# Gated cross-attention and expert mixture in one kernel: weight splits ahead of the context, late GpSimd splits, new work orders

## What is computed

```
q = LN(x) @ Wq;  k = ctx @ Wk;  v = ctx @ Wv          (ctx: 8 x 750 x 512; 8 heads of 64)
a = softmax(q k^T / 8) v, per head                     (scores of 224 x 750 per head)
x = x + tanh(g0) * (a @ Wo + bo)
y = LN(x);  l = y @ gate_w^T + gate_b;  l = l * rsqrt(mean(l^2) + eps) * rms_w
g = top softmax(l / 0.5) entry;  n = g / (g + 1e-6)
x = x + tanh(g1) * n * sum over 8 experts of (gelu(y @ w1[e] + b1[e]) @ w2[e] + b2[e])   (hidden 1024)
```

## Time and profile before

| | |
|---|---|
| runs | 1887.07, 1889.46, 1889.43 us; median 1889.43 |
| profiled execution | 1885.9 us, of which 1884.1 us are the span of the trace |
| DVE, ACT, POOL busy | 71%, 43%, 63% |
| PE, weight loads busy | 97%, 87% |
| mean granted PE clock | 0.99 |

### The profile page before, as it was taken

One profiled execution on the slowest core, in us unless ns is written; L12 is line 12 of the kernel. 1 busy time (PEld: TensorE's weight loads), 2 busy tenths in 40 slices (PEclk: granted clock), 3 DMA queues, 4 the chain that ended last, 5 costly groups with the idle time before them and its releaser, 6 DMA issues.

```text
span 1884.1 us, 32919 instructions
## 1 busy us (share of the span) xinstructions
PE 1821.5 (97%) x10360; PEld 1647.3 (87%) x10360; DVE 1328.9 (71%) x2247; ACT 812.7 (43%) x1570; POOL 1184.9 (63%) x901
## 2 busy tenths in 40 slices
PE   6999999999999869999999999999999999999998
PEld 6999999999999758888888888887888888888887
DVE  6777777777776776766766667579766676676667
ACT  4767666766766543332323323233223233232322
POOL 5525354352544468877777777867777777777742
PEclk9999999999999979999999999999999999999999
DMA  5011111021110213121121211213311112112111
GB/s 174 17 32 59 34 37 55 21 67 29 42 43 13 81 33 122 62 67 56 56 67 45 67 56 56 68 53 116 106 50 62 59 53 67 55 56 66 46 46 51
DMA packets 51804, 110.38 MB, mean 59 GB/s; under 512 B 12953, under 2 KB 25241, under 8 KB 51745
## 3 DMA queue, kind: packets, MB, share of 16 engines
q1 hardware_dynamic: 51744, 109.63, 18.2%
HBM read 98.61 MB, written 11.01 MB: 58 GB/s over the span
## 4 chain that ended last, share of the span: by engine, by line
PE 85%; DVE 9%; issue 3%; ACT 3%; DMA 0%; DVEq 0%; ACTq 0%; SPq 0%
PE bank L683 30%; PE scores L658 28%; PE bank L537 15%; PE scores L601 4%; PE bank L611 4%; PE bank L624 4%; DVE xs L777 1%; DVE neg_max L860 1%; DVE queries L841 1%; ACT queries L1057 1%; DVE acc L944 1%; PE bank L544 1%; DVE probsT L777 0%; PE scores L719 0%; DVE values L777 0%
## 5 line engine op out<-in xcount | busy, mean ns | idle before, releaser
L683 PE MATMUL bank<-w2s,hs 128*128 128x512 f32 x2688 | 621.8, 390 | 5.0 <-DVE acc L944 5.0
L683 PEld LDWEIGHTS bank<-w2s,hs 128*128 128x128 f32 x2688 | 504.3, 188 | 109.5 <-DVE acc L944 7.0
L658 PE MATMUL scores<-xs,w1s 128*128 128x448 f32 x2688 | 562.1, 368 | 4.2 <-DVE h_sum L923 4.2
L658 PEld LDWEIGHTS scores<-xs,w1s 128*128 128x128 f32 x2688 | 507.5, 189 | 49.0 <-issue 2.8
L923 DVE TENSOR_TENSOR h_sum<-scores,h_sum 128x448 f32<-128x448 f32 x448 | 267.2, 620 | 192.2 <-PE scores L658 191.8
L944 DVE TENSOR_TENSOR acc<-bank,acc 128x512 f32<-128x512 f32 x434 | 295.8, 687 | 123.8 <-PE bank L683 114.6
L1183 ACT ACTIVATE h_full<-h_sum,b1T 128x448 f32<-128x448 f32 x256 | 170.9, 668 | 316.9 <-DVE h_sum L923 306.6
L777 DVE TENSOR_TENSOR hs<-h_full,hs 128x448 fp32r<-128x448 f32 x256 | 237.0, 926 | 50.6 <-ACT hs L1184 50.6
L1057 ACT ACTIVATE h_sum<-scores 128x448 f32<-128x448 f32 x64 | 34.9, 545 | 489.9 <-PE scores L658 489.8
L1244 POOL TENSOR_SCALAR probs<-probs,row_inv 112x750 f32<-112x750 f32 x64 | 140.5, 2195 | 164.4 <-DVE row_inv L866 164.4
L1339 POOL CAST w1s<-w_stage 128x768 fp32r<-128x768 f32 x64 | 68.6, 1072 | 182.9 <-PE scores L658 182.9
(11 more groups left out here) (112 smaller groups left out, 2123.8 us busy)
## 6 DMA issues: line engine op xcount, KB each, us to landing
w_stage<-in_L_ffn_w SPq DMA_DIRECT2D x128, 512.0 KB, 3.5
ctx_raw<-in_ctx SPq DMA_DIRECT2D x8, 752.0 KB, 4.6
ctx_raw<-in_ctx SPq DMA_DIRECT2D x7, 748.0 KB, 4.6
xa<-in_x SPq DMA_DIRECT2D x16, 224.0 KB, 2.7
xres<-in_x SPq DMA_DIRECT2D x16, 224.0 KB, 2.7
x_scratch<-xres SPq DMA_DIRECT2D x16, 224.0 KB, 2.3
xt_scratch<-yT SPq DMA_DIRECT2D x16, 224.0 KB, 2.9
x_raw<-xt_scratch SPq DMA_DIRECT2D x4, 896.0 KB, 6.1
```

The source lines that it names most:

```text
L658: mm = pe.matmul(mb[BANK_OF[name]][:, 0:TH], w1s[j % 2][:, s, W_OF[name], kc, :], xs[:, i, m, kc, :], start=n == 0, stop=n == 5)
L683: mm = pe.matmul(bank[:, :], hs[j % 2][:, s, ht, t * P:(t + 1) * P], w2s[j % 2][:, m, ht, :], start=n == 0, stop=n == 5)
```

## The change

1. `N0` stands ahead of `C0.0` and `C0.1` in `HEAD_PLAN`; the rest of the head is reordered.
2. Each context half is loaded as two pairs of column blocks with a semaphore each; a pair is waited for alone.
3. `POOL_PIECES` is (3, 4, 5, 6, 7): ACT and DVE split the first value weights (piece 2), POOL the second key weights (piece 3). POOL begins only when all four context splits of batch 0 and all three splits of the other engines are done. PE waits for each piece at its first use.
4. `BODY_PLAN` and `END_PLAN` are reordered.
5. Between the passes: `POOL_LOWS` = 4, so DVE makes four of the seven lo parts, POOL the last three in step (1, 0, 0), between `w1_part` and `split_w2`. The seven results are spread over steps (1, 0, 0) to (1, 0, 3) by `RESULTS`, and each step's `w2` load follows the first result in it.
6. The gate's third part moves from step j = 2 to j = 3, after sum 1; its Exp moves to product 6 of step 2.

```diff
+RESULTS = {(1, 0, 0): {4: 0, 6: 1}, (1, 0, 1): {3: 2}, (1, 0, 2): {3: 3, 6: 4}, (1, 0, 3): {3: 5, 6: 6}}
+POOL_LOWS = 4
...
-    C0.0 N0 C0.1 L0.0 L0.1 A0.0 N1 K0.0.0 A0.1 K0.1.0 X0 X1 C1.0 N2 C1.1 Q0.0 K0.0.1 N3 N4 V0.0 S0.0 N5 S0.1 R0.0
-    Q0.1 N6 V0.1 V0.2 N7 R0.1 S1.0 M0.0 V0.3 V0.4 K0.1.1 V0.5 S1.1 M0.1
+    N0 C0.0 C0.1 L0.0 L0.1 A0.0 A0.1 K0.0.0 C1.0 N1 X0 C1.1 X1 N2 K0.1.0 K0.0.1 Q0.0 K0.1.1 S0.0 N3 N4 V0.0 Q0.1
+    S0.1 S1.0 R0.0 N5 V0.1 N6 V0.2 M0.0 M0.1 V0.3 V0.4 R0.1 V0.5 N7 S1.1
...
-    D<7 K1.0.0 T0.0 R1.0 Q1.0 R1.1 K1.1.0 T0.1 T0.2 M1.0 S2.0 S2.1 O<0 D0 M1.1 P0 R2.0 T1.0 L<1.0 K1.0.1 O<1 A<1.0
...
-    M7.0 T6.2 S>0.0 R7.1 S>0.1 K>0.1.1 Q>0.1 M7.1 P6 D6 R>0.0 V>0.4 T7.0 T7.1 M>0.0 T7.2 V>0.5 R>0.1 S>1.0 P7
+    D<7 R1.0 K1.0.0 T0.0 R1.1 Q1.0 K1.1.0 T0.1 T0.2 M1.0 S2.0 S2.1 O<0 D0 P0 M1.1 R2.0 L<1.0 A<1.0 T1.0 K1.0.1
...
+    M7.0 T6.1 T6.2 S>0.0 S>0.1 M7.1 Q>0.1 K>0.1.1 V>0.4 R>0.0 P6 D6 T7.0 T7.1 M>0.0 T7.2 V>0.5 R>0.1 S>1.0 P7
...
-    R1.0 D<7 M1.0 T0.0 K1.0.0 R1.1 T0.1 K1.1.0 K1.0.1 T0.2 Q1.0 S2.0 O<0 R2.0 S2.1 M1.1 P0 D0 L<1.0 T1.0 M2.0 T1.1
-    T1.2 R2.1 S3.0 S3.1 M2.1 A<1.0 O<1 P1 D1 Y<0 L<1.1 T2.0 Z T2.1 V1.0 A<1.1 V1.1 R3.0 R3.1 M3.0 V1.2 K1.1.1 S4.0
-    M3.1 T2.2 Q1.1 S4.1 D2 P2 R4.0 G0 V1.3 V1.4 T3.0 T3.1 Y<1 G1 M4.0 S5.0 G2 T3.2 S5.1 R4.1 M4.1 W0.0 G3 D3 P3
-    R5.0 V1.5 R5.1 W0.1 U0 U1 T4.0 T4.1 T4.2 S6.0 R6.0 M5.0 S6.1 M5.1 B0 W0.2 U2 R6.1 U3 P4 W0.3 D4 T5.0 T5.1 M6.0
-    T5.2 S7.0 S7.1 P5 M6.1 R7.0 D5 T6.0 T6.1 U4 M7.0 T6.2 R7.1 W0.4 P6 U5 U6 H0 T7.0 T7.1 T7.2 D6 H1 M7.1 P7 H2 D7
-    H3 H4 O0 O1 W1.0 W1.1 W1.2 L1.0 L1.1 H5 W1.3 A1.0 Y0 A1.1 Y1 W1.4 H6
+    M1.0 R1.0 D<7 T0.0 K1.0.0 K1.1.0 T0.1 K1.0.1 T0.2 R1.1 Q1.0 S2.0 S2.1 R2.0 M1.1 O<0 P0 D0 L<1.0 T1.0 V1.0 R2.1
+    M2.0 V1.1 T1.1 M2.1 T1.2 S3.0 S3.1 O<1 D1 A<1.0 P1 L<1.1 T2.0 A<1.1 Z R3.0 T2.1 Y<0 R3.1 M3.0 K1.1.1 V1.2 M3.1
+    S4.0 T2.2 Q1.1 R4.0 S4.1 P2 G0 D2 V1.3 V1.4 T3.0 Y<1 T3.1 G1 T3.2 M4.0 S5.0 G2 M4.1 S5.1 G3 R4.1 W0.0 P3 V1.5
+    R5.0 R5.1 W0.1 D3 U0 T4.0 T4.1 T4.2 S6.0 R6.0 M5.0 S6.1 M5.1 B0 U1 W0.2 R6.1 P4 U2 W0.3 U3 T5.0 T5.1 M6.0 T5.2
+    D4 S7.0 S7.1 P5 M6.1 R7.0 T6.0 D5 T6.1 T6.2 R7.1 M7.0 U4 P6 U5 U6 W0.4 H0 T7.0 T7.1 D6 T7.2 H1 M7.1 P7 D7 H2
+    H3 H4 O0 O1 W1.0 W1.1 W1.2 L1.0 L1.1 H5 Y0 W1.3 A1.0 A1.1 H6 W1.4 Y1
...
-POOL_PIECES = (2, 4, 5, 6, 7)
+POOL_PIECES = (3, 4, 5, 6, 7)
...
+                for pair in range(2):
...
+                        sp.wait_ge(lo_out["C"], b * KC + (half * 2 + pair - 1))
...
+                    sp.dma_start(dst[:, c, 0:k1 - k0], ctx[b, :, c, k0:k1]).then_inc(ctx_loaded[half][pair], 16)
...
-                    if at(before or g, (0, NE - 1, JS - 1)) and t in (0, 2, 4, 6):
+                    if at(before or g, (0, NE - 1, JS - 1)) and t % 2 == 0 and t // 2 + 3 < POOL_LOWS:
                         split_x(1, t // 2 + 3)
...
-                    if closing and j == 2 and i in (0, 2, 6):
-                        gate(p, (0, 2, 6).index(i))
-                    if at(g, TURN) and i % 2 == 0:
-                        result(0, i // 2)
-                    if at(g, (1, 0, 1)) and i % 2:
-                        result(0, 4 + i // 2)
+                    if closing and j == 2 and i in (0, 2):
+                        gate(p, i // 2)
+                    if closing and j == 3 and i == 1:
+                        gate(p, 2)
+                    if i in results_of(g):
+                        result(0, results_of(g)[i])
...
-                    if closing and j == 2 and i == 4:
+                    if closing and j == 2 and i == 6:
...
+                    if n == 1:
+                        pool.wait_ge(lo_out["C"], KC)
+                        pool.wait_ge(w_lo, len(WEIGHT_PIECES) - len(POOL_PIECES))
...
+                if at(g, (1, 0, 0)):
+                    for i in range(POOL_LOWS, NM):
+                        pool.wait_ge(x_hi, NM + i + 1)
+                        pool.tensor_tensor(xs[:, i, 1], x_source(i), xs[:, i, 0].bitcast(F32),
+                                           ALU.subtract).then_inc(x_split_pool, 1)
                 split_w2(g)
```

More of the change, by code:

```diff
@@ L263, in flamingo_kernel @@
         pool_w_hi, pool_w_lo = sem("pool_w_hi"), sem("pool_w_lo")
-        ctx_loaded = [sem(f"ctx_loaded{i}") for i in range(2)]
+        ctx_loaded = [[sem(f"ctx_loaded{i}{j}") for j in range(2)] for i in range(2)]
         x_loaded = [sem(f"x_loaded{i}") for i in range(2)]
@@ L311, in at, with results_of @@
             return isinstance(g[1], int) and g == there
+        def results_of(g):
+            return RESULTS.get(g, {}) if isinstance(g[1], int) else {}
         def early(g, back):
@@ L355, in load_ctx @@
             def load_ctx(b, half):
[L356 to L361, removed]
-                k0, k1 = HALVES[half]
-                sp.dma_start(dst[:, :, 0:k1 - k0], ctx[b, :, :, k0:k1]).then_inc(ctx_loaded[half], 16)
+                k0, k1 = HALVES[half]
+                for pair in range(2):
+                    if isinstance(b, int) and b == 0:
+                        dst = ctx_head if half else ctx_raw
+                    else:
+                        sp.wait_ge(lo_out["C"], b * KC + (half * 2 + pair - 1))
+                        alone(sp, passed["sp"])
+                        dst = ctx_raw
+                    c = slice(2 * pair, 2 * pair + 2)
+                    sp.dma_start(dst[:, c, 0:k1 - k0], ctx[b, :, c, k0:k1]).then_inc(ctx_loaded[half][pair], 16)
             def load_w(i):
@@ L501, in step @@
                     load_w1(then)
-                if after and not (g[0] == 1 and isinstance(g[1], int) and g[1] == 0 and g[2] < 2):
+                if after and not results_of(g):
                     load_w2(after)
@@ L506, in step @@
                     load_x_raw(1)
-                if at(g, TURN) or at(g, (1, 0, 1)):
-                    for k in (range(4), range(4, PT))[g[2]]:
+                if results_of(g):
+                    for n, k in enumerate(results_of(g).values()):
                         if k + XB < PT:
@@ L688, in _, with weights_split, early_items @@
             pe.wait_ge(consts_set, 3)
[L689 to L693 removed]
+            def weights_split(n):
+                pool_n = sum(1 for k in POOL_PIECES if k < n)
+                if n > pool_n:
+                    pe.wait_ge(w_lo, n - pool_n)
+                if pool_n:
+                    pe.wait_ge(pool_w_lo, pool_n)
+            def early_items(plan):
+                for item in plan:
+                    if item[0] in "KQV" and item[1] == 0:
+                        weights_split(WEIGHT_PIECES.index((f"w{item[0].lower()}", item[2])) + 1)
+                    elif item[0] == "T":
+                        weights_split(6)
+                    yield item
+            for item in early_items(HEAD_PLAN):
                 make(item, 0, bank_of["head"])
[L695 to L696 removed]
             def batch(name, plan, b):
[L699 to L700 removed]
+                if name == "first":
+                    for item in early_items(plan):
+                        make(item, b, bank_of[name])
+                    weights_split(len(WEIGHT_PIECES))
+                else:
+                    for item in plan:
+                        make(item, b, bank_of[name])
             batches(pe, batch)
@@ L1084, in hi @@
                         return
-                    act.wait_ge(ctx_loaded[half], 16)
+                    act.wait_ge(ctx_loaded[half][pair], 16)
                     copy(ctxT[:, 0, c, k0:k1], src[:, c, 0:k1 - k0]).then_inc(hi_out["C"], 1)
@@ L1276, in handle @@
                         pool.wait_ge(in_psum["V"], number(("V", 0, 1, 5 if half else 3), b))
-                        pool.wait_ge(ctx_loaded[half], (b + db) * 16 + 16)
+                    pool.wait_ge(ctx_loaded[half][pair], (b + db) * 16 + 16)
                     alone(pool, passed["pool"])
```

36 lines of the change are left out of this document (17 added, 19 removed).

## The result

The changed kernel takes **1876.99 us** in the median of 4 runs (1875.12 to 1878.46), against 1888.59 us (1887.07 to 1889.46) before: a ratio of 0.9939, interval 0.9923 to 0.9955. I had forecast 1871.5 within 1861 to 1882. So it is faster, by 11.6 us instead of 17.9. The profiled execution took 1877.21 us, its span is 1875.4 us: 8.7 less than the 1884.1 of before.

What follows compares the result with a forecast made beforehand. PE, busy 1821.5 of 1884.1 us, was taken as the bound, leaving only idle time and low clock to win. Head -4.0, middle 0, last batch -4.5, gate -3.1, turn -6.3 gave -17.9: 1871.5 us, range 1861 to 1882.

Steps and rivals of the forecast that it cites:

- Head, forecast -4.0: Start to first T0.0: earlier first matmul and POOL held back win 5.5 us, less 1.5 for PE's clock; bounds -1 to -7.
- the 1.5 us taken off for PE's clock: Head: 1.5 us deducted because three short PE pauses before 20 us may cost it the clock.
- the signs named: Head: first matmul at 9 to 10 us, POOL's split behind 20, second-half ctxT subtractions under 1 each, T0.0 at about 41.
- Middle batches, forecast 0: Seven middle batches: PE's 0.7 us wait for the queries stays and the new order costs nothing; bounds -6 to +4.
- my slower rival: Middle batches: T1.0's drain behind A<1.0 stalls PE seven times; at 3.2 us per batch, 1894 us; chance 0.05.
- a sign of being wrong: Middle batches: a change of over 0.5 us each would show the prediction wrong.
- Last batch, forecast -4.5: Last batch: 1.5 to 2 us at T5.0, U4's 3.1 at P6, partly taken back by T7's drain; bounds 0 to -9.
- POOL holds the last batch: Rival, last batch: M5.1 and M6.1 end as before, U4's gain lost behind U5 and U6; 1876 us; chance 0.15.
- Gate, forecast -3.1 in the second pass: Second layer beside the gate: six small instructions leave the full step, winning 3.1 us in pass two, nothing in pass one.
- Turn, forecast -6.3: Between the passes: DVE loses three lo parts and two results, PE's h_sum waits go, two product sets take 17.0 us.
- The second rival: Turn: POOL's three lo parts block DVE, 6.3 us, giving back all the turn's gain; 1877.8 us; chance 0.1.

Runs made afterwards that it cites:

- the second one of before: The kernel before, with no edit, profiled once more: 1887.77 us, its head 2.67 us longer than in the first trace.
- ctx_whole: The changed kernel with ScalarE's copy of each context pair waiting for both pairs of its half: median 1876.83 us.
- three_results: The changed kernel with the old middle order, the gate behind product 0, U5 and U6 later, and result 1 moved to the turn's second step: 1870.33 us.

## Why the prediction was right or wrong

The total held, faster and inside the range. The steps did not all hold; they missed in both directions. That the total came out inside the range is in part luck: the head gave 2.3 us or more beyond its term, and the middle, the last batch and the turn together fell short by some 11.

- **Head, forecast -4.0: too small.** It is -6.3 between the first two traces, -9.0 against the second one of before. The second lies outside my bounds (-1 to -7). The landing was mis-sized. I took 7.5 us for the first pair, and ScalarE copied it at 5.41 us, right behind the weights' copy, so it was there by then; the first matmul came at 7.72. Making the pair late again (ctx_whole) cost 1.3 us at T0.0. Whether the 1.5 us taken off for PE's clock were lost is not resolved: the granted clock from the first matmul to T0.0 reads 1.00 (0.95 before), yet the first six matmuls took 2.22 us, as long as twelve of the same shape did behind 37 us. Of the signs named, POOL's first weight split behind 20 us (20.34) and context subtractions under 1 us (0.94 and 0.93) came; the first matmul and T0.0 (39.4) came earlier than the 9 to 10 and 41 named.
- **Middle batches, forecast 0: wrong, +3.3.** The step that failed is "between K>0.0.1 and S>0.0 the new order keeps the same PE items and the same DVE items ahead of Q>0.0; it stays". It doesn't: V>0.3 now stands ahead of T6.1, and R7.1 ahead of Q>0.0. Taking the last third back brought that wait back to 0.7 us but only 0.15 of the 0.49 us per batch; the rest lies further up in the order, in places not singled out. I also walked the plan only for waits that the trace of before showed as long. The values' wait was 0.2 us and grew by 0.4. It was inside the bounds I gave (-6 to +4), and well under my slower rival, whose place (the drain of T1.0 behind A<1.0) shows no wait. At 0.48 us per batch the change stayed just inside the 0.5 that I had named as a sign of being wrong.
- **Last batch, forecast -4.5: nothing** (+1.0 between the first two traces, inside its spread). Half of the mechanism came: the probsT wait shrank from 7.9 to 1.0 us, and T5.0 and T6.0 started 4.6 and 4.4 us earlier on the clock, more than the 3.0 by which the batch itself began earlier. At T7.0 only 0.2 of these 1.6 us were left. What failed is "then U4's 3.1 at P6, of which the drain of T7 behind U4, U5 and U6 takes back some". It wasn't the drain of T7: U5 and U6 now stood beside POOL's scaling M7.1, which took 3.94 us instead of 2.17, and PE, pausing again, ran T7, H1 and P7 at a low clock (granted 0.70 from 680 to 690 us, 0.79 before). My rival "POOL holds the last batch" is what came about, with a block between DVE and POOL in the place of POOL's order. Moving U5 and U6 away gave back some 1.7 us; what holds the rest of the 4.5 is open.
- **Gate, forecast -3.1 in the second pass: right in the profile, by chance.** Part 3 had moved from under one split of POOL to within 0.1 us of the start of the next one's cast. Where it comes behind that, pass 2 is 567.8 to 569.4 us, about before's 568.9. The term should have been about half of 3.1. In the first pass the 3.1 us were won and lost again behind, as forecast: from the first second layer to the turn's first product it is 568.16 us, against 568.49 before, with a wait of PE of 1.4 us for acc in front of the turn.
- **Turn, forecast -6.3: -3.5 in pass 1, with the first gate.** The two sets of products at the turn went from 23.38 to 20.25 us, not to 17.0. The failed step is "PE's two waits for h_sum and the low clock behind them go": the waits stay, 0.85 and 1.76 us in the changed kernel. The first was 2.49 us before, the second 1.73, so only the first shrank. I counted instructions taken off DVE at their own length, and overlooked that the second wait stands behind two subtractions of hs that take 3.33 us beside a w1 split of POOL. The trace of before has them too, DVE's row and PE's:

```profile
1302.08 3.33 DVE L777 TENSOR_TENSOR hs<-h_full,hs 128x448 fp32r<-128x448 f32 x2
1306.00 5.21 PE L658 MATMUL scores<-xs,w1s 128*128 128x448 f32 x24 [1.73 <-DVE h_sum L923]
```

Where result 1 no longer stood in front of them (three_results), that wait fell to 0.57 us. The second rival named the block of DVE by POOL, but for the three moved parts; beside those DVE's additions from PSUM kept 0.6 us each, and what was blocked were the hs parts, by a split that was there before. Its price was too high (6.3, where 2.8 of my term are missing), and the move to POOL is still worth 1.4 us.

- **Sum.** -6.3 to -9.0, +3.3, 0, -3.5, and -3.3 or about 0 in the second pass: -6.5 to -12.5, around -9.5. The medians give -11.6, and -10.7 to -11.0 against those of before in the later sessions. The 2 us between are less than the spread of the head in two traces; they are not resolved further.

## What to carry to other kernels

Put a column of stage lengths beside the total: it showed 3.3 us of loss in a part that looked untouched, and a gain that was lost again two steps on. When an instruction is moved, ask which long instruction of the other engine it will start beside, and with what margin; a margin of less than 0.1 us is a coin toss, and a few elements can then cost 2 us and the clock behind it. In an order written by hand that runs seven times, half a microsecond per round is worth more than most of the stalls at the edges.

## What the runs showed that I had not expected

- The two-input DVE instruction on 128x7 elements took 0.17 us with POOL idle, 0.66 to 0.71 beside a POOL cast, and 2.27 to 2.28 us in the four traces in which it started 0.12 us behind a POOL subtraction of 2.4 us. The second trace of before has a case of its own, 2.02 us. The block lasts as long as the rest of the other engine's instruction, whatever the size of the blocked one.
- The one-input instruction L1047, also 128x7, took 0.17 us when it started up to 0.09 us ahead of POOL's cast, and 0.97 to 1.04 us, to the end of the cast, when it started up to 0.09 us behind its start.
- It goes both ways: POOL's scaling of 112x750 took 2.17 us alone, 3.02 beside one DVE subtraction of xs, and 3.94 beside three.
- PE's clock after the wait of 6.5 us for the last layer norm came back at different moments. From the first transpose behind the wait to the first second layer the same instructions took 13.41 us at a granted clock of 0.77 in the changed kernel, and 11.90 at 0.88 with the old middle order, 1.5 us that no edit explains:

```profile
703.82:717.23 13.41, 13.41 (x57) 12.25 (x57) 7.25 (x11) 4.97 (x9) 6.00 (x6) 0.77 0.38 114
```

```profile
699.62:711.52 11.90, 11.90 (x56) 10.97 (x57) 7.00 (x12) 5.20 (x10) 4.10 (x4) 0.88 0.46 129
```
